# A fused decoder layer on one Trainium2 core: values in halves, a transposition ahead of the adds, other joined pairs, and TensorE's attention program written out

## The reference

```python
x = layernorm(x + attn(x, w_qkv, w_out, b_out))      # 16 heads of 32, softmax over 2048 keys
x = layernorm(x + xattn(x, ctx, ctx, W_out))         # one head over 77 context rows
x = layernorm(x + ffn(x, ...))                       # fake-quantised gated FFN, 1408 wide

def attn(x):                                         # per head h
    q, k, v = split(einsum('bnd,ed->bne', x, w_qkv)) # -> heads
    dots = einsum('bhnd,bhmd->bhnm', q, k) * 32 ** -0.5
    out = einsum('bhnm,bhmd->bhnd', softmax(dots), v)
    return einsum('bnd,ed->bne', out, w_out) + b_out
```

## Time and profile before

| | us |
|---|---|
| median of 3 runs (1947.2 to 1951.31) | 1948.23 |
| the profiled execution | 1950.18 |
| its span, first to last instruction | 1948.4 |
| 32 chunks, from the first `gather` to the last | 1091.56 |
| granted clock of TensorE, mean over the span | 0.967 |

### The profile page before, as it was taken

One profiled execution on the slowest core, in us unless ns is written; L12 is line 12 of the kernel. 1 busy time (PEld: TensorE's weight loads), 2 busy tenths in 40 slices (PEclk: granted clock), 3 DMA queues, 4 the chain that ended last, 5 costly groups with the idle time before them and its releaser, 6 DMA issues. The chain is left out here.

```text
span 1948.4 us, 38894 instructions
## 1 busy us (share of the span) xinstructions
PE 1814.7 (93%) x14516; PEld 845.0 (43%) x14516; DVE 1456.9 (75%) x1579; ACT 1448.6 (74%) x1572; POOL 161.3 (8%) x131
## 2 busy tenths in 40 slices
PE   8999996999999999999999999999939996899786
PEld 6777772333333333333333333333327774444332
DVE  5443435888888888888888888888826776688687
ACT  5343445999999999999999999999905654555475
POOL 0000000000000000000000000000011220000164
PEclk9999998999999999999999999999969996899898
DMA  8655654536446364463555354463653520133274
GB/s 293 224 202 199 221 194 166 109 91 151 92 113 145 75 145 113 89 159 80 114 140 108 88 151 94 110 148 75 143 184 135 182 93 1 60 141 156 80 281 167
DMA packets 111553, 268.57 MB, mean 138 GB/s; under 512 B 7956, under 2 KB 26516, under 8 KB 101780
## 3 DMA queue, kind: packets, MB, share of 16 engines
q1 hardware_dynamic: 98324, 193.05, 27.4%
q0 software_dynamic: 9216, 67.11, 18.6%
q10 hardware_dynamic: 3968, 7.86, 1.1%
HBM read 115.95 MB, written 84.93 MB: 103 GB/s over the span
## 5 line engine op out<-in xcount | busy, mean ns | idle before, releaser
L783 DVE TENSOR_TENSOR dve_sum<-dve_sum,probs 128x2048 f32<-128x2048 f32 x320 | 732.8, 2290 | 80.7 <-ACT probs L699 73.1
L699 ACT ACTIVATE probs<-score_others,shift_now 128x1536 f32<-128x1536 f32 x384 | 622.0, 1620 | 0.0
L840 PE MATMUL score_first<-q_parts,k_parts 32*128 32x512 f32 x1542 | 494.1, 425 | 24.2 <-DMA v_group<-v_scratch 11.6
L840 PE MATMUL score_others<-q_parts,k_parts 32*128 32x512 f32 x4626 | 499.0, 426 | 0.0
L840 PEld LDWEIGHTS score_first<-q_parts,k_parts 32*128 32x128 f32 x1542 | 245.0, 183 | 492.2 <-ACT probs L698 288.0
L868 PE MATMUL mixed_ps<-probs,v_group 128*32 128x512 f32 x3072 | 395.9, 603 | 2.9
L698 ACT ACTIVATE probs<-score_first,shift_now 128x512 f32<-128x512 f32 x384 | 291.1, 758 | 43.0 <-PE score_others L840 43.0
L840 PEld LDWEIGHTS score_others<-q_parts,k_parts 32*128 32x128 f32 x4626 | 252.6, 183 | 2.2
L699 ACT ACTIVATE probs_joined<-score_others,shift_now 128x1536 f32<-128x1536 f32 x128 | 199.9, 1562 | 0.0
L812 POOL DMA_DIRECT2D probs_joined<-probs_joined x64 | 55.2, 863 | 1040.7 <-PE mixed_ps L868 1010.7
L868 PEld LDWEIGHTS mixed_ps<-probs,v_group 128*32 128x32 f32 x3072 | 67.1, 108 | 160.2 <-issue 110.0
(11 more groups left out here) (206 smaller groups left out, 2181.9 us busy)
## 6 DMA issues: line engine op xcount, KB each, us to landing
probs_joined<-probs_joined POOLq DMA_DIRECT2D x64, 1024.0 KB, 8.6
k_parts<-k_scratch SPq DMA_DIRECT2D x36, 512.0 KB, 4.8
q_parts<-q_scratch SPq DMA_DIRECT2D x33, 512.0 KB, 7.8
o_scratch<-out_parts SPq DMA_DIRECT2D x33, 512.0 KB, 2.8
h_scratch<-h SPq DMA_DIRECT2D x6, 2816.0 KB, 8.1
h<-h_scratch SPq DMA_DIRECT2D x6, 2816.0 KB, 10.5
k_scratch<-parts SPq DMA_DIRECT2D x32, 512.0 KB, 3.6
q_scratch<-parts SPq DMA_DIRECT2D x32, 512.0 KB, 2.7
```

The source lines that it names most:

```text
L699: nc.scalar.activation(block_probs(k)[:, CH:HPG * CH], score_others[n % 2][:], ACT.Exp, bias=shift[:, c:c + 1], scale=SCALE).then_inc(prob ...
L783: nc.vector.tensor_tensor(total[:], first[:], block_probs(k)[:], ALU.add).then_inc(dve_added, 1)
L840: last = nc.tensor.matmul(out, k_parts[rows, a, k * P:(k + 1) * P], q_parts[c][rows, b, :], start=t == 0, stop=t == len(TERMS) - 1)
```

## The change

- **Values in halves.** `VALUES_AT` gives way to `VALUE_HALVES`: how many halves (256 of the 512 query columns) of value blocks a step does. Steps 2, 3, 5, 6, 8, 9, 11, 12, 14 and 15 do two, steps 4, 7, 10 and 13 do three. Where a block is cut by a step's end, its four matmuls of 512 columns become four of 256 in one step and four of 256 in the next; this happens to blocks 3, 4, 5, 10, 11 and 12.
- **`finish` ahead of the adds.** VectorE does `take_shift` and `finish` before the first add of the chunk, not after it.
- **Other pairs.** Blocks 4 and 5, and 9 and 10, are joined by DMA, in place of 8 and 9, and 10 and 11. Still 12 blocks are added by VectorE, in 11 adds, and still three `sums`. TensorE waits for the DMA's own semaphores; GpSimd no longer waits for the DMAs inside its loop.
- **Buffers.** `normal` goes (the product is written over `mixed`, and `gather` waits for the split of it), and `out_parts` has one buffer in place of two.
- **TensorE's program** is written out for all 32 chunks, with constant waits, in place of a loop of 16 turns; the two scores that were computed past the last chunk are gone.

The diff, cut to its core:

```diff
-    JOINED = (8, 9, 10, 11)
-    ADDED = [k for k in range(KB) if k not in JOINED]
...
+    PAIRS = ((4, 5), (9, 10))
+    TO_SUMS = (0, 1)
+    ADD_ORDER = [k for k in range(KB) if not any(k in pair for pair in PAIRS)]
...
-    VALUES_AT = [[], [], [0], [1, 2], [3], [4, 5]] + [[k] for k in range(6, KB)]
+
+    VALUE_HALVES = (0, 0, 2, 2, 3, 2, 2, 3, 2, 2, 3, 2, 2, 3, 2, 2)
+    HALF = CH // 2
...
-        normal = [sb(f"normal{u}", [P, CH], F32) for u in range(2)]
-        out_parts = [sb(f"out_parts{u}", [P, 2, CH], F32R) for u in range(2)]
+        out_parts = sb("out_parts", [P, 2, CH], F32R)
...
-                            if k in JOINED:
+                            i = pair_of(k)
+                            if i in TO_SUMS:
                                 act.wait_ge(sums_done, it * CPB + c + 2)
...
-                            elif ADDED.index(k) >= P_RING:
-                                act.wait_ge(dve_added, (it * CPB + c + 1) * ADDS + max(ADDED.index(k) - P_RING, 1))
...
+                            elif SINGLE.index(k) >= P_RING:
+                                act.wait_ge(dve_added, (it * CPB + c + 1) * ADDS + added_at(SINGLE[SINGLE.index(k) - P_RING]))
...
-                    v.wait_ge(normal_done, 1 + f)
+                    v.wait_ge(lo_done, 2 + f)
                     nc.vector.tensor_copy(mixed[:], mixed_ps[:]).then_inc(mixed_copied, 1)
...
-                    nc.vector.tensor_tensor(normal[u][:], mixed[:], inverse[:], ALU.mult).then_inc(normal_done, 1)
+                    nc.vector.tensor_tensor(mixed[:], mixed[:], inverse[:], ALU.mult).then_inc(normal_done, 1)
                     v.wait_ge(normal_done, 1 + f + 1)
...
+                    v.wait_ge(stored, 1 + 16 * f)
...
                         total = dve_sum[c % 2]
+
+                        take_shift(it if c == 0 else it + 1, (c + CPB - 1) % CPB)
+                        finish(it, c)
                         for a in range(ADDS):
-                            k = ADDED[a + 1]
-                            n = c * KB + k
-                            if a == 1:
-
-                                take_shift(it if c == 0 else it + 1, (c + CPB - 1) % CPB)
-                                finish(it, c)
                             if a == ADDS - 1:
...
-                        for i in range(2):
-
-                            pool.wait_ge(mixed_done, (it + 1) * BLOCKS + c * KB + JOINED[2 * i + 1] + 1)
+                        for i, pair in enumerate(PAIRS):
+
+                            pool.wait_ge(mixed_done, (it + 1) * BLOCKS + c * KB + pair[1] + 1)
                             pool.sem_inc(may_join, 1)
...
-                        for i in range(2):
-                            pool.wait_ge(dma_joined[i], 16 * (it * CPB + c + 1))
-                            pool.sem_inc(joined, 1)
...
+                    if at < len(TO_SUMS):
+                        part = probs_paired[TO_SUMS[at]][0]
+                        if f > 0:
+                            pe.wait_ge(joined[TO_SUMS[at]], 16 * f)
...
+                def values(f, k, halves):
+
+                    pe.wait_ge(probs_done, EXPS + (f * KB + k + 1) * 2)
                     if k == 0:
 
-                        pe.wait_ge(sums_read, 1 + turn * PAIR + c + 1)
+                        pe.wait_ge(sums_read, 1 + f + 1)
+                    lo, hi = halves[0] * HALF, (halves[-1] + 1) * HALF
                     for j in range(HPG):
-                        last = nc.tensor.matmul(mixed_ps[j * HD:(j + 1) * HD, :], v_group[:, k, j * HD:(j + 1) * HD],
-                                                block_probs(k)[:, j * CH:(j + 1) * CH], start=k == 0, stop=k == KB - 1)
-                    last.then_inc(mixed_done, 1)
+                        last = nc.tensor.matmul(mixed_ps[j * HD:(j + 1) * HD, lo:hi], v_group[:, k, j * HD:(j + 1) * HD],
+                                                block_probs(k)[:, j * CH + lo:j * CH + hi], start=k == 0, stop=k == KB - 1)
+                    if halves[-1] == 1:
+                        last.then_inc(mixed_done, 1)
...
-                with pe.Fori(0, TURNS) as turn:
-                    for c in range(PAIR):
-                        for step, blocks in enumerate(VALUES_AT):
-                            score(turn, c * KB + step + AHEAD)
-                            for at in ((0,), (1, 2))[step] if step < 2 else ():
-                                sums(turn, c, at)
-                            for k in blocks:
-                                values(turn, c, k)
...
+                for f in range(CHUNKS):
+                    done = 0
+                    for step, halves in enumerate(VALUE_HALVES):
+                        if f * KB + step + AHEAD < CHUNKS * KB:
+                            score(f * KB + step + AHEAD)
+                        for at in SUMS_AT[step] if step < len(SUMS_AT) else ():
+                            sums(f, at)
+                        for k in range(KB):
+                            now = [half for half in range(2) if done <= 2 * k + half < done + halves]
+                            if now:
+                                values(f, k, now)
+                        done += halves
```

More of the change, by code:

```diff
@@ L608, in attend, with pair_of, added_at @@
         w_in, w_hi_done, w_lo_done = sem("w_out_in"), sem("w_out_hi_done"), sem("w_out_lo_done")
[L609 removed]
+        stored = sem("stored")
         KV_UP = 16 * 2
         def block_probs(k):
[L615 removed]
+            i = pair_of(k)
+            return probs[SINGLE.index(k) % P_RING] if i is None else probs_paired[i][PAIRS[i].index(k)]
+        def pair_of(k):
+            return next((i for i, pair in enumerate(PAIRS) if k in pair), None)
+        def added_at(k):
+            return max(ADD_ORDER.index(k), 1)
         with nc.Block() as block:
@@ L831, in score @@
+                def score(n):
+                    f, k = n // KB, n % KB
+                    if k % KPP == 0 and f % CPB == 0:
+                        pe.wait_ge(kv_in[k // KPP], (f // CPB + 1) * KV_UP)
                     if k == 0:
-                        pe.wait_ge(q_in[c], 16 * (turn + 1))
-                    pe.wait_ge(probs_done, EXPS + turn * (2 * TURN_BLOCKS) + (n - 1) * 2 + 1)
+                        pe.wait_ge(q_in[f % 2], 16 * (f // 2 + 1))
+                    if n > 0:
+                        pe.wait_ge(probs_done, EXPS + (n - 1) * 2 + 1)
@@ L839, in score, with sums @@
                             out = score_first[:] if h == 0 else score_others[n % 2][:, (h - 1) * CH:h * CH]
-                            last = nc.tensor.matmul(out, k_parts[rows, a, k * P:(k + 1) * P], q_parts[c][rows, b, :],
+                            last = nc.tensor.matmul(out, k_parts[rows, a, k * P:(k + 1) * P], q_parts[f % 2][rows, b, :],
                                                     start=t == 0, stop=t == len(TERMS) - 1)
                     last.then_inc(scores_done, 1)
-                def sums(turn, c, at):
-                    f = turn * PAIR + c
+                def sums(f, at):
```

82 lines of the change are left out of this document (35 added, 47 removed).

## The result

| | before | after |
|---|---|---|
| median of the runs, us | 1948.21 (1947.2 to 1951.31, 4 runs) | 1918.39 (1916.18 to 1920.16, 4 runs) |
| the profiled execution | 1950.18 | 1916.18 |
| its span | 1948.4 | 1914.4 |
| first `gather` to last, 32 chunks | 1091.56 | 1060.93 |
| ahead of it / behind it, in the span | 320.9 / 535.9 | 318.3 / 535.1 |

The ratio is 0.9844, with a 95% interval of 0.9827 to 0.9861. The forecast was 1911.3 with a range of 1902 to 1928: faster, as said, and 7.1 us short of the forecast. By the medians the gain is 29.8 us, by the two profiled executions 34.0. The profiled run of after was the lowest of its four, and that of before was 2.0 above its median.

The account below looks back on a forecast made before the run. An uneven deal of TensorE's work holding ScalarE was taken to set the 34.11 us chunk. 32 x (34.11 - 33.05) = 33.9, plus 3 at the end, gives 36.9 us: from 1948.23 to 1911.3, range 1902 to 1928.

Parts of the forecast that it names:

- The rule of steps: Attention steps: TensorE may be 0.24 us late before ScalarE waits; a one-block step recovers 0.12; any excess holds ScalarE.
- The chunk: One of 32 attention chunks: from 34.11 to 33.05 us (32.98 to 33.3), being 32.95 plus 0.1 for cutting.
- the sign: What would show the forecast right: `gather` to `gather` 33.0 to 33.1 us; wrong if the chunk is outside 32.8 to 33.5.
- What cutting costs: 24 short passes a chunk from six cut blocks: 0.1 us a chunk, within 0.03 to 0.36.
- Rival 1: Short passes cost more than 0.015 us each, so steps 5, 6, 11, 12 hold ScalarE: 1927 or 1946; chance 0.11.
- Transposition first: Transposition of the sums no longer waits behind VectorE's first add: up to 0.2 us, inside the step rule's 32.95.
- The add that moved: VectorE's first add after `finish` still fits, 0.65 us left before the next `gather`; cost 0.
- Rival 2: VectorE becomes the bound and `gather` is late: chunks 33.4 to 33.7 us, time 1922 to 1933; chance 0.09.
- Joins: Second join lands some 2 us ahead of need, so TensorE's wait of about 0.2 us for it goes.
- The program written out: TensorE's program straight for all 32 chunks, some 90 instruction packets: counted as 0 per chunk.
- rival 3: Instruction fetching stalls TensorE at about 90 boundaries: slower than before, 2001 at 1 us each; chance 0.07.
- The end: Behind the last chunk: two scores gone (about 1.0 us) and the last join's wait about 2 shorter; 3 us (1 to 5).

Follow-up runs that it names:

- whole blocks further apart: Changed kernel with uncut value blocks and its two double steps moved to steps 5 and 10: 1932.94 us, ratio 0.9918.
- the loop: Changed kernel with TensorE's program again a loop of 16 turns of two chunks, GpSimd relaying the joins: 1915.96 us, ratio 0.9827.
- the run: Changed kernel with eight more blocks a chunk issued as two half sets each in the same step: 1920.86 us, ratio 0.9863.
- the second series: The changed kernel measured again, unaltered, beside the second group of experiments: 1919.03 us, ratio 0.9845.
- the third join: Changed kernel with pairs (3, 4) and (5, 6), a third DMA adding the two results, and one `sums` fewer: 2107.54 us, ratio 1.0815.

## Why the prediction was right, and where its sizes were off

*What bounds it.* Right for the kernel before. The rule of steps (0.24 of slack, 0.12 recovered, the rest holds ScalarE) forecast 34.1 for before; with whole blocks further apart it said 33.6, and 33.66 was measured; with halves all but one of ScalarE's gaps went. The gap left is 0.4 (12.0 / 31) where 0.5 was forecast, and the four of less than 0.1 don't show as idle time. Steps were forecast at 1.89 and 2.32 and came at 1.90 and 2.33.

*The chunk.* Forecast 33.05, measured 33.15 in the mean and 33.19 without the last, shorter one; over 32 chunks that is 4.3 us more than forecast, and a typical chunk (33.17) lies just outside the 33.0 to 33.1 that was named as the sign. The step that failed is the start of the account: it went by ScalarE's held time (32.95) and checked TensorE only by its work (32.8), taking it as if it never stood. Once ScalarE was free, TensorE became the bound, and two waits on VectorE that had been in ScalarE's shadow counted in full:
- step 0 takes 1.98, since the first `sums` starts at 717.67, behind the copy out of `mixed_ps` (716.92 + 0.69), not at 716.70 + 0.89: 0.08;
- step 2 takes 2.00, since `values` of block 0 start at 722.43, 0.14 behind the end of the transposition (721.57 + 0.72), and not at 721.43 + 0.90: 0.10.

The two together are 0.18 to 0.19 a chunk. The other 14 steps are 0.01 longer each than the prices of the prediction, in the mean, which is the rest of the way from 32.8 to 33.17 (what cutting costs is in it).

The second wait stood in the kernel before too (15.4 us in 30 chunks for TensorE's loads, the usual 0.36 of each included), inside a chunk that ScalarE set. How much such a wait costs depends on more than the two engines' times: of the 0.10 in step 2 all but 0.01 goes with the written-out program, since in the loop, with the same order and halves, the step takes 1.91 in the mean of 30 chunks. Copying the tile out by halves was not tried.

*What cutting costs.* The term was 0.1 a chunk within 0.03 to 0.36. At 0.0015 a short pass, 24 of them are 0.04: the lower bound, taken from the float32 matmuls of 128 columns, was nearly the value, and the upper one, from the scores' loads, held for another kind of matmul only. Rival 1 falls. The overhead of about 60 cycles for each small matmul that the Trainium skill states ("TensorEngine Tiling (Array Packing)", Instruction Overhead) gives, as an estimate at 2.4 GHz, 0.4 us for 16 added passes; the run shows 0.05. (The prediction's own estimate from that page, 0.3 us a chunk for 12 added passes, is 9.6 us over 32 chunks, or 6.4 above a sum that already holds 0.1 a chunk, and not 8.)

*Transposition first.* The mechanism was right and the size wrong: "up to 0.2 us", read from a chunk in which a late join stood in for it. Measured, the old order costs 0.32 a chunk with halves and 0.27 without, 9 to 10 us of chunks in all. The row that should have been used is VectorE's own distance from `gather` to transposition, 5.08, against TensorE's: `sums` end 4.65 after `gather` (716.92 to 721.57) when nothing is late, so 0.4 is what TensorE would wait. The 4.65 is from the changed kernel's trace. It did not spoil the sum, because 32.95 already supposed the wait gone.

*The add that moved.* Right for the changed kernel: VectorE's wait ahead of `gather` was forecast at 0.5 to 0.7 and is 0.92 (28.6 / 31), that ahead of the transposition about 2 and is 1.7. Rival 2 falls. But "ScalarE's tiles come free 3 us or more ahead of need" was true only through the new pairs: with the old ones the same move costs 27 us. The prediction costed that at nothing without naming this cover.

*Joins.* Right: read 10.7 us after the issue, some 2.7 ahead of need by the median landing, and a single load in 31 chunks that is put down to the join, with 0.4 idle ahead of it, hardly more than the usual 0.36. In the last chunk it waited 0.97 (see below). What it did not see is how thin the ground is. It counted the join's wait as 0.2 us to be won; issued one step later, with the old pairs, the same transfer costs up to 4.5 a chunk.

*The program written out.* Forecast 0 a chunk. No wait that the trace names is a fetch, and rival 3 falls, but the edit isn't free: the thirty middle chunks are 33.17 in the mean (33.16 in the second series) against 33.11 in the loop. By steps, in the mean of these 30 chunks, step 2 takes 2.00 where the loop has 1.91, step 0 takes 1.99 where the loop has 2.03, step 9 takes 1.91 against 1.90, and the rest agree within 0.01. So what the written-out form costs sits in one wait, that for the transposition: TensorE starts 0.15 us after its end in all 30 chunks, and 0.05 in the loop. In step 0 the loop is the slower, where its joins come by way of GpSimd. The delay is the same to 0.01 in every chunk, while 95 packets over 31 chunks fall at changing places, so fetching is an unlikely cause. The two forms give the number waited for in different ways, as a constant or from a register; that this is the cause was not tested. Only step 9 has single chunks at 1.97, in about one of four, and whether those are fetches was not tested either.

The Trainium skill ("Runtime: NRT & Kernel Launch", Instruction fetch mechanics) has it that a taken branch to a page outside the current window forces a fetch, which is one reason to unroll, and that a straight program hides most of its fetching. Here the loop, with a turn every 66 us, shows 4 instruction packets in 1020 us against 95 for the straight program, and none at all from 430 to 1380 us, so its branches there forced no fetch, and the loop is the faster of the two by 0.05 us a chunk. The straight program's gain is only the two scores it can leave out.

*The end.* Forecast 3 us. The last chunk is 32.15 in place of 34.01, of which 0.9 is the general gain of a chunk and 1.0 the missing scores. From there to the transposition of the last sums it takes 6.14 us (1379.26 to 1385.40) where it took 6.68. The join's wait shrank from 1.39 to 0.97 and not by 2, since this last transfer took 9.8 us to its reader and not 8; behind it the sums ran at the lower of TensorE's two clocks in both kernels (1.94 and 1.72 us for eight matmuls that take 1.06 elsewhere). So 1.5 us of the 3 came.

*The sum.* The terms asked for 33.9 + 3 = 36.9 us. In the two traces 29.6 came from the chunks (30.6 less the 1.0 of the missing scores) and 1.5 from the end, 31.1 together, where 5.8 are missing: 4.3 in the chunks and 1.5 at the end, as above. The two profiled executions differ by 34.0, since 2.6 us more lie ahead of the chunks, in what the change does not touch. The medians differ by 29.8. That the profiled run's own time, 2.0 above its median, was taken over as a fixed distance was sound for before and says nothing of after, whose profiled run was 2.2 below its own.

## What to carry to other kernels

When two engines are both near the bound, lay out their work step by step: what counts is how far one step may run over before the other engine stands, and half a block in twice as many steps may fit where a whole one does not. Then go through the sum once more with the freed engine taken away, because waits that were in its shadow now count in full. And before costing an edit at nothing, ask which other part of the same change holds its cover: here the same two edits gave 35 us or cost 96, depending mainly on which blocks a DMA adds.

## What the runs showed of the hardware

- Two joins of 1 MB issued 3.8 us apart landed in a median of 9.4 us and at most 12.9 (old pairs with halves and `finish` first). Issued 4.0 us apart in the kernel before, they took 8.6 and at most 10.5; issued five blocks apart, 8.0 and at most 10.3. The loads of K and V fall among them in all three.
- The granted clock of TensorE fell after an idle stretch. With the third join TensorE stood 3.66 us ahead of 710.68. From 709.6 to 716.2 the granted clock (seventh number, ahead of the DMA share) was 0.50, the lower of its two levels (1.2 and 2.4 GHz), and the eight matmuls behind the wait took 1.93 where they take 1.06 elsewhere.

```profile
690.00:706.00 16.00, 16.00 (x196) 6.27 (x192) 15.48 (x7) 15.99 (x17) 1.72 (x2) 1.00 0.84 176
709.60:716.20 6.60, 5.38 (x28) 1.27 (x28) 0.07 (x1) 0.00 (x0) 0.00 (x0) 0.50 0.01 1
716.40:720.00 3.60, 3.02 (x36) 1.30 (x40) 3.17 (x9) 3.60 (x4) 0.00 (x0) 1.00 0.02 5
```

- So a late transfer is paid for twice. With the third join the chunks were 5.9 us longer each than in the changed kernel (1248.43 against 1060.93 for 32). TensorE was idle for 4.8 us of a chunk (1093.34 busy of 1248.43), 3.9 of it the wait for the join (102.5 / 26) and 0.9 the wait for ScalarE behind it. It was also busy 1.1 longer a chunk (1093.34 against 1058.72), although 0.86 us of sums was gone. The two chunks behind the first that had a clock of 1.00 were busy 32.4 to 32.5 us, the mean of all is 34.2, so the lower clock cost about 1.7 a chunk.
- A float32 set of four matmuls of 256 columns costs half of one of 512, to 0.0015 us a pass, with four matmuls side by side in the array.
- The start of a matmul that had waited for VectorE's transposition came 0.15 us after the transposition's end where TensorE's program was written out (the changed kernel), and 0.05 where it was a loop (the same kernel with the loop).
- The two traces of the changed kernel differ by 1.9 us ahead of the attention and 1.2 behind it, while its 32 chunks repeat within 0.4 us.
